# Routed rows that carry their own weight, one summed row per token, and sums added on GpSimd, in a fused attention and mixture-of-experts kernel

## The reference, cut to what matters

```python
xn = _layernorm(x)
# attention: q = xn @ wq, c_kv = xn @ w_down, k and v = c_kv @ w_up, rope, causal softmax, @ wo
scores = sigmoid(xt @ gate_w.T)
top_scores, top_idx = top_k(scores, 2)
top_scores = top_scores / (sum(top_scores) + 1e-20) * 2.5
combine = sum(one_hot(top_idx, 8) * top_scores[..., None], axis=1)
y = einsum('eth,ehd->etd', silu(h) * u, w2)          # of each expert
routed = einsum('etd,te->td', y, combine)
shared = silu(xt @ sw1) * (xt @ sw3) @ sw2
return x + attention(xn) + routed + shared
```

## Time and profile before

| | us |
|---|---|
| median of 3 runs | 752.09 (751.59 to 752.86) |
| the profiled execution | 751.67 |
| its span, first to last instruction | 749.9 |

### The profile page before, as it was taken

How to read it: one execution, slowest core, us unless ns; L and a number is a source line. 1 busy time by engine, 2 the same in 40 slices (tenths; PEclk the granted TensorE clock), 3 DMA queues, 4 the chain that set the end, 5 groups by cost and what they waited for, 6 DMA issues and landing times.

```text
span 749.9 us, 15632 instructions
## 1 busy us (share of the span) xinstructions
PE 704.7 (94%) x4554; PEld 631.8 (84%) x4554; DVE 645.1 (86%) x1756; ACT 588.5 (78%) x1472; POOL 496.2 (66%) x450
## 2 busy tenths in 40 slices
PE   4788978999999999999999999999999999999975
PEld 3777767888888999999999999999999999987764
DVE  6577999999998888888888888988898889888886
ACT  3666667887878888888888888888988898887751
POOL 2544456778877677767876777677766767676620
PEclk9999999999999999999999999999999999999997
DMA  9553222543434444644464445544555454223201
GB/s 291 167 157 102 82 63 98 163 136 110 127 104 157 123 146 137 200 129 150 132 194 137 151 131 161 170 153 128 160 170 157 126 158 130 69 65 113 86 28 57
DMA packets 61396, 99.67 MB, mean 133 GB/s; under 512 B 9840, under 2 KB 33568, under 8 KB 61312
## 3 DMA queue, kind: packets, MB, share of 16 engines
q1 hardware_dynamic: 57904, 89.35, 39.2%
q0 software_dynamic: 3408, 9.33, 3.3%
HBM read 72.14 MB, written 26.51 MB: 132 GB/s over the span
## 4 chain that ended last, share of the span: by engine, by line
PE 68%; DVE 13%; POOL 6%; issue 5%; ACT 5%; DMA 1%; DVEq 0%; ACTq 0%; POOLq 0%
PE qk_proj L445 13%; PE u_acc L445 12%; PE scores L445 12%; PE out_acc L445 11%; PE ffn L445 10%; PE probs_t L548 6%; DVE acc L1235 2%; POOL swapped L910 2%; ACT swapped L760 1%; DVE rot L1181 1%; POOL rot L918 1%; POOL qk_lo L925 1%; DVE pt_lo L1212 1%; PE ffn L629 1%; POOL xs_sorted L941 1%
## 5 line engine op out<-in xcount | busy, mean ns | idle before, releaser
L910 POOL TENSOR_TENSOR swapped<-swapped,sin_t 128x512 f32<-128x512 f32 x128 | 164.9, 1288 | 180.3 <-DVE rot L1188 147.4
L925 POOL TENSOR_TENSOR qk_lo<-rot,qk_hi 128x512 fp32r<-128x512 f32 x128 | 163.3, 1294 | 11.2 <-ACT qk_hi L769 11.0
L780 ACT ACTIVATE probs<-scores,nbias 128x512 f32<-128x512 f32 (+3 forms) x256 | 134.9, 527 | 33.9 <-DVE nbias L1197 31.8
L1212 DVE TENSOR_TENSOR pt_lo<-probs_t,pt_hi 128x512 fp32r<-128x512 f32 x238 | 117.7, 495 | 48.0 <-ACT pt_hi L791 47.7
L760 ACT ACTIVATE swapped<-qk_proj 64x512 f32<-64x512 f32 x256 | 151.7, 592 | 6.2 <-PE qk_proj L445 1.6
L791 ACT ACTIVATE pt_hi<-probs_t 128x512 fp32r<-128x512 f32 x238 | 105.0, 441 | 44.6 <-PE probs_t L548 36.3
L1197 DVE CUSTOM_DVE_ANT_0 scores<-scores,mask 128x512 f32<-128x512 f32 (+3 forms) x256 | 125.3, 490 | 7.4 <-PE scores L445 1.6
L1235 DVE SCALAR_TENSOR_TENSOR acc<-out_acc,rsum,acc 128x256 f32<-128x256 f32 x256 | 111.0, 476 | 2.1
L548 PE MATMUL probs_t<-ident,probs 128*128 128x128 f32 x604 | 105.8, 274 | 7.4 <-DVE pt_lo L1212 6.8
L445 PE MATMUL scores<-qk_hi 128*128 128x512 f32 (+3 forms) x256 | 94.5, 369 | 3.5 <-ACT probs L780 3.2
L1181 DVE TENSOR_TENSOR rot<-qk_proj,cos_t 128x512 f32<-128x512 f32 x128 | 87.5, 684 | 10.1 <-ACT swapped L760 9.1
(11 more groups left out here) (182 smaller groups left out, 1837.6 us busy)
## 6 DMA issues: line engine op xcount, KB each, us to landing
wt<-expert_parts SPq DMA_DIRECT2D x39, 704.0 KB, 4.5
wt<-expert_parts SPq DMA_DIRECT2D x39, 512.0 KB
raw_a<-in_attn SPq DMA_DIRECT2D x8, 768.0 KB, 5.7
xs_sorted<-u_lo SPq DMA_DIRECT2D x3, 1670.5 KB, 9.1
xs<-xs_sorted SPq DMA_DIRECT2D x39, 128.5 KB, 2.9
expert_parts<-split SPq DMA_DIRECT2D x8, 352.0 KB, 2.3
expert_parts<-raw_f SPq DMA_DIRECT2D x8, 352.0 KB, 2.5
acc<-in_x SPq DMA_DIRECT2D x4, 512.0 KB, 6.7
```

Of the source, the lines that this page charges most:

```text
L780: ac.activation(probs[:, m % 2, PR_AT[i]:PR_AT[i] + n], s_bank[i % 2][:, 0:n], ACT.Exp, bias=nbias[:, m % 2, i:i + 1], scale=-1.0, accum_o ...
L910: pool.tensor_tensor(swapped[:, which, :], swapped[:, which, :], sin_t[:, :], ALU.mult).then_inc(sinm_ok[which], 1)
L925: pool.tensor_tensor(qk_lo[:, m % 2, which, :], rot[:, which, :], f32(qk_hi[:, m % 2, which, :]), ALU.subtract).then_inc(rlo_ok[which], 1)
L1212: ve.tensor_tensor(pt_lo[:, c], turn_bank(m, j)[:, 0:n], f32(pt_hi[:, c]), ALU.subtract).then_inc(ptlo_ok, 1)
```

## The change

- A row of `xs_sorted` gets a second extra value, its weight. `route_weights` writes the weights of the first choice straight into `xn` and those of the second into `topw`; POOL copies the second ones over before the second half of the scatters. It moves from step 4 to step 2 on DVE, and the first scatter waits for it.
- `row_homes` copies the weights to `share` as well, and takes the larger of the row's number and of a number from 1 to 128 that is the partition's own, so that padding rows go to 128 different rows.
- ACT's `result` multiplies each row by its weight while it copies.
- `ys_tokens` gets one row for each token, is filled with zeros by an SP DMA in step 0 (`zero_sums`), and `result_home` scatters with `compute_op=ALU.add`, so that the DMA adds to what stands there.
- `results_in` loads one row per token, one DMA for a group. `add_routed` is one POOL instruction for a group of two tiles, at the end of POOL's steps 57 to 63, groups 4 to 7 (batches 2 and 3) first. DVE's `add_head` of batches 2 and 3 in the last eight slots waits for POOL's adds to them; POOL's adds to batches 0 and 1 wait for `add_head` of slots 57 and 59. The output is written in the order of batches 0, 2, 1, 3.

```diff
-DX = D + 1
+DX = D + 2
-        ys_d = nc.dram_tensor("ys_tokens", (1 + TOP_K * TT * P, D), F32).ap()
+        ys_d = nc.dram_tensor("ys_tokens", (1 + P + TT * P, D), F32).ap()
-        BACK = {F_LAST + 3: (0, 1), F_LAST + 4: (2, 3), F_LAST + 5: (4, 5), F_LAST + 6: (6, 7)}
-        ADDS = {(58, EARLY): 0, (59, EARLY): 1, (60, EARLY): 2, (61, EARLY): 3, (61, MIDDLE): 4, (62, EARLY): 5,
-                (62, MIDDLE): 6, (63, MIDDLE): 7}
+        BACK = {F_LAST + 3: (4, 5), F_LAST + 4: (6, 7), F_LAST + 5: (0, 1), F_LAST + 6: (2, 3)}
+        ADDS = {57: (4,), 58: (5,), 59: (6,), 60: (7, 0), 61: (1,), 62: (2,), 63: (3,)}
@@ SP
+            def zero_sums():
+                sp.dma_start(ys_d[1:].rearrange("(t p) d -> p t d", p=P),
+                             mask[:, 0:D].unsqueeze(1).to_broadcast([P, 1 + TT, D])).then_inc(st_zsum, 16)
-                for i in range(2):
-                    sp.dma_start(xn[:, 2 * g + i, 0:D], rows[0][i]).then_inc(ld_rows[g], 16)
-                    sp.dma_start(back[2 * g + i], rows[1][i]).then_inc(ld_rows[g], 16)
+                sp.dma_start(xn[:, 2 * g:2 * g + 2, 0:D],
+                             ys_d[1 + P:][2 * g * P:2 * (g + 1) * P].rearrange("(i p) d -> p i d",
+                                                                               p=P)).then_inc(ld_rows[g], 16)
-            for b in range(B):
+            for b in (0, 2, 1, 3):
                 sp.wait_ge(add_ok, NT * (SLOTS - 8 + 2 * b + 2))
-                sp.wait_ge(yadd_ok, (b + 1) * NT * TOP_K)
+                sp.wait_ge(yadd_ok, groups_added(b))
@@ ACT, result
-                ac.activation(ysb[:, t % 2, :], f_bank[:, 0:D], ACT.Copy).then_inc(yev_ok, 1)
+                ac.wait_ge(home_ok, t + 1)
+                ac.activation(ysb[:, t % 2, :], f_bank[:, 0:D], ACT.Copy,
+                              scale=share[:, t % 4:t % 4 + 1]).then_inc(yev_ok, 1)
@@ POOL, result_home
-                                        in_=ysb[:, t % 2, :], in_offset=None).then_inc(st_y[t % 2], 16)
+                                        in_=ysb[:, t % 2, :], in_offset=None,
+                                        compute_op=ALU.add).then_inc(st_y[t % 2], 16)
@@ POOL, row_homes
-                pool.tensor_copy(home[:, t % 4:t % 4 + 1], xs[:, t % 2, D:DX]).then_inc(home_ok, 1)
+                pool.tensor_copy(share[:, t % 4:t % 4 + 1], xs[:, t % 2, D + 1:DX])
+                pool.tensor_scalar(home[:, t % 4:t % 4 + 1], xs[:, t % 2, D:D + 1], first_id[:, 0:1], None,
+                                   ALU.max).then_inc(home_ok, 1)
+            def add_routed(group, s):
+                pool.wait_ge(ld_rows[group], 16)
+                pool.wait_ge(add_ok, NT * (last_head(group, s) + 1))
+                a = acc[:, 2 * group:2 * group + 2, :]
+                pool.tensor_tensor(a, a, xn[:, 2 * group:2 * group + 2, 0:D], ALU.add).then_inc(yadd_ok, 1)
@@ DVE, route_weights
-                for k in range(TOP_K):
-                    last = ve.scalar_tensor_tensor(out=topw[:, k, :], in0=best[:, k, :], scalar=0.5 * ROUTED_SCALE,
+                for k, to in enumerate((xn[:, :, D + 1], topw[:, :])):
+                    last = ve.scalar_tensor_tensor(out=to, in0=best[:, k, :], scalar=0.5 * ROUTED_SCALE,
                                                    in1=tsum[:, 1, :], op0=ALU.mult, op1=ALU.mult)
@@ DVE, add_head
-                need(ve, yadd_ok, steps["back"])
+                if m >= SLOTS - 8 and 2 * b in ADD_ORDER[:4]:
+                    ve.wait_ge(yadd_ok, groups_added(b))
@@ DVE: add_routed is gone
-                for k in range(TOP_K):
-                    for i in range(2):
-                        ...
-                        ve.scalar_tensor_tensor(out=acc[:, t, :], in0=of, scalar=topw[:, k, t:t + 1], in1=acc[:, t, :],
-                                                op0=ALU.mult, op1=ALU.add).then_inc(yadd_ok, 1)
```

More of the change, by code:

```diff
@@ L270, in scatter_steps, with last_head, groups_added @@
             return range(n, n + SCATTERS.get(s, 0))
-        BACK = {F_LAST + 3: (0, 1), F_LAST + 4: (2, 3), F_LAST + 5: (4, 5), F_LAST + 6: (6, 7)}
-        EARLY, MIDDLE, END = range(3)
-        ADDS = {(58, EARLY): 0, (59, EARLY): 1, (60, EARLY): 2, (61, EARLY): 3, (61, MIDDLE): 4, (62, EARLY): 5,
-                (62, MIDDLE): 6, (63, MIDDLE): 7}
+        BACK = {F_LAST + 3: (4, 5), F_LAST + 4: (6, 7), F_LAST + 5: (0, 1), F_LAST + 6: (2, 3)}
+        ADDS = {57: (4,), 58: (5,), 59: (6,), 60: (7, 0), 61: (1,), 62: (2,), 63: (3,)}
+        ADD_ORDER = [g for at in sorted(ADDS) for g in ADDS[at]]
+        def last_head(g, s):
+            return max(m for m in range(s - 1) if where(m)[1] == g // 2)
+        def groups_added(b):
+            return 1 + max(ADD_ORDER.index(g) for g in (2 * b, 2 * b + 1))
         def moves_rows(s):
@@ L413, in _ @@
                     attn_weights(1)
+                if s == PICK_AT:
+                    zero_sums()
                 if r == 5 and q + 1 < PAIRS:
@@ L986, in _ @@
                 row_homes(ffn_tile(s + 1))
+                for group in ADDS.get(s, ()):
+                    add_routed(group, s)
                 if s == -LEAD + 1:
@@ L992, in _ @@
         def _(ve):
-            steps = {"route": 0, "inv": 0, "adds": 0, "shared": 0, "back": 0}
+            steps = {"route": 0, "inv": 0, "adds": 0, "shared": 0}
             def step(ins):
@@ L1281, in add_shared @@
                 steps["shared"] += 1
-            def add_routed(g):
-                ve.wait_ge(ld_rows[g], 16 * PER_GROUP)
-                need(ve, add_ok, steps["adds"])
-                for k in range(TOP_K):
-                    for i in range(2):
-                        t = 2 * g + i
-                        of = xn[:, t, 0:D] if k == 0 else back[t]
-                        if k == 1:
-                            ve.wait_ge(yadd_ok, steps["back"] + i + 1)
-                        ve.scalar_tensor_tensor(out=acc[:, t, :], in0=of, scalar=topw[:, k, t:t + 1], in1=acc[:, t, :],
-                                                op0=ALU.mult, op1=ALU.add).then_inc(yadd_ok, 1)
-                steps["back"] += PER_GROUP
-            def add_group(s, at):
-                if (s, at) in ADDS:
-                    add_routed(ADDS[s, at])
             for s in range(-LEAD, SLOTS + 1):
@@ L1309, in _ @@
                     expert_parts(n)
-                add_group(s, EARLY)
                 sorted_parts(f)
@@ L1321, in _ @@
                     place_tiles()
+                    route_weights()
                 if s == PLACE_AT + 1:
@@ L1326, in _ @@
                     place_owners()
-                    route_weights()
                 pt_parts(s, 3)
```

26 lines of the change are left out of this document (11 added, 15 removed).

## The result

| | before | after |
|---|---|---|
| median of the runs, us | 751.88 (751.59 to 752.86, 4 runs) | 742.0 (740.12 to 743.84, 4 runs) |
| the profiled execution, us | 751.67 | 740.12 |
| its span, us | 749.9 | 738.2 |

The ratio is 0.9878, 95% interval 0.9855 to 0.99. The forecast was 741.6 us with a range of 739.5 to 748.5. The same kernel measured again on another occasion (e1) had 742.16 us.

What follows compares the result with a forecast made beforehand. PE, busy 94% of the span, bounds the routed steps; DVE paces routing and its adds lie on the tail's path. Tail gain 11.3 less 0.8 gives 10.5 us: 741.2 profiled, 741.6 as median, range 739.5 to 748.5.

Steps and rivals of the forecast that it cites:

- The tail, steps 58 to 60: Steps 58 to 60: without the adds on DVE each is as step 57, 9.11 us; gain 3.76 us.
- Steps 61 to 63: Last three steps, adds gone and PE at full clock: 7.8, 6.35 and 5.6 us, gaining 2.2, 2.2 and 2.5.
- the likelier of the two cases: Last three steps: PE keeps its full clock, tail gain 11.3 us; with the lower clock as before, 7.9 us.
- The end: After the last `u_lo`: without the adds, some 3.4 us to the last `acc` in place of 4.07, gaining 0.65 us.
- the last output DMA follows as before: End of the kernel: the last output DMA follows the last `acc` as before, so the 0.65 us gained there stays.
- POOL: Tail: POOL's adds, 1.29 us each, fit into 2.65 us of idle time before `sin_product` and leave 1.35 us.
- rival 2: Steps 58 to 60: POOL's adds reach the path and the gain there goes, 745.4 us; chance 0.10.
- the port rule: Tail: DVE instructions with two SBUF inputs and POOL's SBUF reads exclude each other; an add 0.5 us later would stop `rotate`.
- The routed steps: Steps with a routed tile: adding scatter (landing taken as 8 us), scaled copy and `row_homes` stay hidden; steps remain 10.54 us.
- rival 3: Routed steps: the adding scatter lands later than 10.5 us after issue and POOL waits; about 778 us at 11.5; chance 0.09.
- Routing and zeros: Early steps: `route_weights` widens PE's gap in step 2 to about 2.75 us, costing 0.8 us; `zero_sums` costs nothing.

Runs made afterwards that it cites:

- e5: The changed kernel with four unused DVE instructions put back at the old place of the adds in each of steps 58 to 60: 747.64 us.
- e12: The changed kernel with three small tiles allocated earlier, POOL's `rotate` moved to DVE in steps 54 to 60, and the last batch's output in two DMAs: 749.33 us.
- e4: The changed kernel with `route_weights` placed behind `u_parts` in step 2: 742.46 us.
- e3: The changed kernel with the adds back on DVE at their former places, one instruction for a group: 743.57 us.
- e10: The changed kernel with two more POOL instructions ahead of the add in each of steps 57 to 59: 746.63 us.
- e2: The changed kernel without POOL's eight adds and the waits for them, scatter and loads kept: 741.72 us.
- e9: The changed kernel with one more POOL instruction ahead of the add in each of steps 57 to 59: 745.43 us.
- e7: The changed kernel with a plain scatter in place of the adding one: 740.15 us.
- e8: The changed kernel with ACT's copy of the expert result not scaled by the weight: 742.15 us.
- e11: The changed kernel with `sums`, `rsum` and `std` declared earlier, which puts other buffers at other addresses: 743.84 us.
- e6: The changed kernel with four unused DVE instructions put back at each of the five former places of adds in steps 61 to 63: 753.55 us.

## Why the prediction was right

**The tail, steps 58 to 60.** Right to 0.02 us: 3.74 against 3.76. The method was to take the step without an add (57) as the model of those with one. e5 undoes it: 4.4 us come back, more than 3.74. The four instructions there take 2.08 us and not 1.67, beside a POOL add that before did not have, which is 0.4 us in each step and more than enough for the difference.

**Steps 61 to 63.** Forecast 7.8, 6.35 and 5.6 us, measured 7.51, 6.13 and 5.92. The clock stayed full, the likelier of the two cases. The sum, 6.9 us, was met by 7.1. In step 61 PE's own work was as summed, 6.78 us (6.7), but of its wait for `u_lo` only 0.73 us lies in the step (7.51 less 6.78; taken 1.1). In step 62 it is 5.02 us (5.50), in step 63 it is 4.17 us, where halving the time at the lower level had given 3.5: that term was mis-sized by 0.67 us, and waits of 1.75 us in place of 2.1 gave half of it back. The reason for the clock was right in kind, since a fall is there in all three traces with the full work of the adds on DVE and in none of the others. The path to it was not. The prediction argued from a wait that goes and from shorter steps with the same matmuls; e12 has a wait of 2.94 us and steps as long as before, and keeps the clock. Nor did it see that the adds of steps 58 to 60 are enough for the fall of step 61, as e5 shows. So the full clock was forecast rightly by odds rather than by a mechanism that the rows held, and part of the sum is luck: some executions of before can't have had both falls.

**The clock as a general rule.** Waits of 1.76 us went without a fall, one of 1.74 us in e4 had one. At the turn to step 61, 1.38 and 1.37 us had one (before, e5), and 1.38, 1.52 and 2.94 us had none (e3, e10, e12). A single wait's length does not decide it, and what does stays open. The prediction held this open with two cases and chances, and that was as far as the rows went.

**The end.** The last `acc` ends 3.42 us after `u_lo`, as forecast (3.4). The timeline of DVE in after:

```profile
732.91 1.66 DVE L1261 SCALAR_TENSOR_TENSOR acc<-out_acc,rsum,acc 128x256 f32<-128x256 f32 x4 [1.07 <-PE out_acc L453]
```

It ends at 734.57, and the span ends 3.65 us later; before it was 3.34. So between these two traces 0.34 us was gained and not 0.65. That is no sign that the term "the last output DMA follows as before" was wrong: e2, e9 and e10, with the changed order of the output, have 3.34 to 3.35 us as well, and e1 has 3.64. And in e1, where the lower clock starts at 734.9, the last `acc` ends 3.61 us after `u_lo` and not 3.42. The two traces can't tell whether 0.65 or less was gained.

**POOL.** The add takes 1.20 us (taken 1.29) and leaves 1.50 us idle (forecast 1.35); e2 shows it to be free. Of the price of rival 2, 3.8 us in three steps, e10 shows 3.1 us, and 4.05 with step 61: two more instructions put 0.3, 1.4 and 1.4 us on the steps, and 1.0 on step 61. But it begins sooner than the idle time says: in e9 at one more instruction, through `rotate`, which the add holds up, and not through POOL's queue. There the port rule, which the prediction had set against the change, was the better guide. The expectation of e12 left it out, and e12 lost most of the gain.

**The routed steps.** The adding scatter takes 1.62 us on POOL, 0.59 more than the earlier trace rows, within the 1.9 us that I had left. It lands after 4.2 us (at most 7.2). I took 8, much too long, and rival 3 needed 10.8. The scaled copy is 0.09 us longer than the earlier trace rows, the second instruction of `row_homes` is hidden. What I had not foreseen is the 0.77 us in 38 steps, 20 ns a step. e7 and e8 rule out the scatter and the copy, and e11 one layout; the cause stays open.

**Routing and zeros.** PE's idle time in step 2 is 2.58 us (forecast 2.75), and the clock fell (0.90 in that step). The price was 0.15 us in steps 1 to 4 and not 0.8: steps 2 and 3 became 0.84 and 0.30 us longer and step 4 1.0 us shorter. `zero_sums` lands after 7.5 us (estimated 12), hidden.

**In sum.** The mechanism of the adds on DVE's path was right, the full clock came as forecast without a mechanism that the runs bear out, and the sizes cancelled in part: terms of +0.77 (routed steps), +0.31 (end) and +0.13 us (steps 54 to 57) that I did not have stand against -0.65 (steps 1 to 4) and -0.2 (steps 61 to 63). Without the start-up the spans differ by 10.19 us, the medians by 9.9, against 10.5.

## What to carry to other kernels

When an engine's work sits on the path only in some steps, take the same steps without it as the model: that gave 0.02 us over three steps. Making the work small comes before moving it: four instructions turned into one were worth about 9.4 us of 11.2 (with the clock that came back in that trace), the other engine 1.8. And before work goes to GpSimd, look not only for idle time there but for DVE instructions with two SBUF operands beside it, and keep the distance between them.

## What the runs showed of the hardware

- DVE and POOL instructions with two SBUF operands hold each other up, and those of DVE lose more by it. A `rotate` of 0.69 us took 1.14 us with a POOL instruction over its first 0.58 us (e9), and 1.69 us beside POOL's `rot_parts` (e12); four instructions took 5.38 us in place of 1.67 to 2.08 beside five POOL adds, and these 6.30 in place of 5.76 (e6).
- An indirect DMA that adds costs little more than one that writes: 1.62 against 1.08 us of POOL for its issue, 4.2 against 3.8 us to land, for 128 rows of 256 values.
- The last output in two DMAs of 256 KB instead of one of 512 KB ended 0.7 to 1.1 us earlier, counted from the last `acc` (e12, one trace; 2.59 against 3.34 to 3.65 us).
- PE waits of one length had a clock fall beside them in one kernel and not in another: 1.76 us without, 1.74 with (e4); 1.38 us with the earlier trace rows, 1.38 without (e3); and 2.94 us without (e12).
- The same 2720 matmuls at full clock took 405.03 us in one kernel and 405.70 to 405.80 in others, with PE busy throughout (e7, e8, e11).
